# Latent attention: two transfers for the rows of a maximum in place of four, the first half's query rows shared by two queues, narrow maxima one slot later

## The reference

```python
Wdkv = x @ latent_w + latent_b                                   # [b, t, 36]: keys and values at once
q = jnp.einsum('btc,hcl->bhtl', x, Wd_w) + Wd_b[None, :, None, :]    # 16 heads, 36 wide
scores = jnp.einsum('bhtl,bsl->bhts', q, Wdkv) / sqrt(d_head)
scores = jnp.where(causal[None, None, :, :], scores, -jnp.inf)
attn = jax.nn.softmax(scores, axis=-1)
y = jnp.einsum('bhts,bsl->bhtl', attn, Wdkv)
return jnp.transpose(y, (0, 2, 1, 3)).reshape(b, t, h * 36) @ out_w + out_b
```

## Time and profile before

| what | value |
|---|---|
| median of 3 runs | 3344.71 us |
| the profiled execution | 3344.79 us, span 3343.1 us |
| PE busy | 2818.7 us (84%) |
| DVE busy | 2042.5 us (61%) |
| ACT busy | 1147.9 us (34%) |
| POOL busy | 805.4 us (24%) |
| stretch of the latent attention's pairs | 2143 to 3181 us |

### The profile page before, as it was taken

How to read it: one execution, slowest core, us unless ns; L and a number is a source line. 1 busy time by engine, 2 the same in 40 slices (tenths; PEclk the granted TensorE clock), 3 DMA queues, 4 the chain that set the end, 5 groups by cost and what they waited for, 6 DMA issues and landing times. The chain is left out here.

```text
span 3343.1 us, 53892 instructions
## 1 busy us (share of the span) xinstructions
PE 2818.7 (84%) x15208; PEld 1921.7 (57%) x15208; DVE 2042.5 (61%) x5177; ACT 1147.9 (34%) x2094; POOL 805.4 (24%) x1092
## 2 busy tenths in 40 slices
PE   5999999867888887799999988577887887787877
PEld 4777777644555555577777764334544454454453
DVE  6777777667777776677777763444544444454433
ACT  2111111146666665211111113244344433434332
POOL 1232232235555555222323210011001000000100
PEclk8999999968888888899999989688988888899888
DMA  3000000000000000200000000001001000101000
GB/s 124 0 0 0 0 0 0 1 1 2 3 2 3 2 2 3 92 0 0 0 0 0 0 1 0 27 28 34 23 26 30 28 23 28 33 23 32 23 1 25
DMA packets 31481, 52.02 MB, mean 16 GB/s; under 512 B 6914, under 2 KB 12290, under 8 KB 31236
## 3 DMA queue, kind: packets, MB, share of 16 engines
q1 hardware_dynamic: 31236, 48.96, 4.8%
HBM read 17.93 MB, written 2.10 MB: 6 GB/s over the span
## 5 line engine op out<-in xcount | busy, mean ns | idle before, releaser
L555 DVE SCALAR_TENSOR_TENSOR moe_acc<-moe_ps,moe_comb,moe_acc 128x512 f32<-128x512 f32 x896 | 661.2, 744 | 176.2 <-PE moe_ps L304 169.6
L2059 DVE CUSTOM_DVE_ANT_0 attn_masked<-attn_psm,attn_causal 128x1024 f32<-128x1024 f32 (+7 forms) x512 | 369.5, 756 | 456.3 <-PE attn_psm L1758 456.2
L1961 ACT ACTIVATE attn_probs<-attn_pse 128x512 f32<-128x512 f32 (+1 forms) x640 | 319.4, 554 | 470.6 <-PE attn_pse L1773 469.2
L304 PE MATMUL moe_ps<-moe_Wg,moe_xh 128*128 128x512 f32 x1024 | 329.9, 404 | 24.7 <-DVE moe_Wu L501 24.7
L335 PE MATMUL moe_ps<-moe_Wd,moe_ih 128*128 128x512 f32 x1024 | 337.9, 411 | 0.0
L304 PE MATMUL moe_ps<-moe_Wu,moe_xh 128*128 128x512 f32 x1024 | 337.6, 411 | 0.0
L1699 POOL TENSOR_SCALAR_AFFINE_SELECT attn_probs<-attn_probs 128x256 f32<-128x256 f32 (+1 forms) x192 | 94.6, 493 | 973.9 <-ACT attn_probs L1961 972.8
L1789 PE MATMUL attn_psy<-attn_probs,attn_V 128*64 128x512 f32 (+3 forms) x1536 | 328.2, 565 | 0.0
L1758 PE MATMUL attn_psm<-attn_kS,attn_qS 108*128 108x512 f32 (+3 forms) x672 | 214.2, 423 | 126.0 <-DMA attn_qS<-attn_qL 77.8
L454 POOL TENSOR_SCALAR moe_part<-consts,moe_pick,moe_prob 128x8 f32<-128x8 f32 x256 | 97.4, 395 | 753.6 <-ACT moe_prob L389 753.6
L1758 PEld LDWEIGHTS attn_psm<-attn_kS,attn_qS 108*128 108x128 f32 x672 | 123.0, 211 | 258.1 <-DVE attn_mx L2059 134.0
(11 more groups left out here) (208 smaller groups left out, 4747.4 us busy)
## 6 DMA issues: line engine op xcount, KB each, us to landing
attn_qS<-attn_qH SPq DMA_DIRECT2D x256, 72.0 KB
attn_qS<-attn_qL SPq DMA_DIRECT2D x128, 72.0 KB
moe_stageg<-in_w_gate SPq DMA_DIRECT2D x8, 512.0 KB, 7.0
moe_stageu<-in_w_up SPq DMA_DIRECT2D x8, 512.0 KB, 8.0
moe_stageg<-in_w_down SPq DMA_DIRECT2D x8, 512.0 KB, 3.6
out<-X SPq DMA_DIRECT2D x1, 2048.0 KB, 8.7
attn_qS<-attn_mh SPq DMA_DIRECT2D x64, 4.0 KB
attn_qS<-attn_ml SPq DMA_DIRECT2D x64, 4.0 KB
```

The costliest lines, as they stand in the source:

```text
L304: last = pe.matmul(expert_bank[j % 4][:, :], a[q][:, :], w[b][:, cols], start=k == 0, stop=k == 2)
L555: dve.scalar_tensor_tensor(acc[:, q, r, :], expert_bank[j % 4][:, :], comb[:, q, r, e:e + 1], acc[:, q, r, :], ALU.mult, ALU.add).then_inc ...
L1961: act.activation(probs[:, ring(q, u), c, HALF - n:HALF], e_part(k, HALF - n, HALF), ACT.Exp, scale=SCORE_SCALE).then_inc(p_ready, 1)
L2059: dve.tensor_tensor_reduce(masked[:, k % 2, 0:n], m_all[:, base:base + n], causal[:, SEQ - n:SEQ], 1.0, NEG, ALU.add, ALU.max, mx[:, q, v: ...
```

## The change

The two tiles `qS` of a pair's two heads become one tile with the heads side by side. With that one transfer carries a row of the maxima for both heads: two transfers instead of four, and the high row's is issued as soon as `mh` is there, ahead of the wait for `ml`. Of the six transfers of the first half, POOL issues the three of head 0 (at the place between its select of unit 8 and that of unit 9) and SP the three of head 1. The maxima are given a new order: slot 0 holds one wide maximum only, the narrow ones follow from slot 1 on, slot 3 holds two of them, and a maximum waits for the one before it of its own width, wherever that stands.

```diff
-        qS = [[sb(f"qS{q}{c}", [KROWS, SEQ], F32R) for c in range(2)] for q in range(2)]
+        qS = [sb(f"qS{q}", [KROWS, 2, SEQ], F32R) for q in range(2)]
...
-        QUERY_TILE = [8 * c + j for c in range(2) for wide, small in ((7, 1), (6, 2), (5, 3), (4, 0)) for j in (wide, small)]
+        WIDE = [(0, 7), (0, 5), (1, 7), (1, 5), (0, 6), (0, 4), (1, 6), (1, 4)]
+        NARROW = [(c, j) for j in (3, 2, 1, 0) for c in range(2)]
+        MAXIMA = [WIDE[0:1], (WIDE[1], NARROW[0]), (WIDE[2], NARROW[1]), (NARROW[2], WIDE[3], NARROW[3]),
+                  (WIDE[4], NARROW[4]), (WIDE[5], NARROW[5]), (WIDE[6], NARROW[6]), (WIDE[7], NARROW[7])]
...
+        def query_rows(eng, q, h, c, arrived):
+            s = HALVES[h]
+            half, rows = slice(s * HALF, (s + 1) * HALF), slice(c * LAT, (c + 1) * LAT)
+            for part, src in enumerate((qH, qH, qL)):
+                eng.dma_start(f32(qS[q][part * LAT:(part + 1) * LAT, c, half]), f32(src[q][rows, half])).then_inc(arrived, 16)
...
                 def maxima(m, q):
+                    sp.wait_ge(mh_ready, after(m))
+                    sp.dma_start(f32(qS[q][STACK:STACK + 1, :, :]), f32(mh[:, q, :])).then_inc(m_in, 16)
                     sp.wait_ge(ml_ready, after(m))
-                    for c in range(2):
-                        sp.dma_start(f32(qS[q][c][STACK:STACK + 1, :]), f32(mh[8 * c:8 * c + 8, q, :])).then_inc(m_in, 16)
-                        sp.dma_start(f32(qS[q][c][STACK + 1:STACK + 2, :]), f32(ml[8 * c:8 * c + 8, q, :])).then_inc(m_in, 16)
+                    sp.dma_start(f32(qS[q][STACK + 1:STACK + 2, :, :]), f32(ml[:, q, :])).then_inc(m_in, 16)
...
                 def queries(p, q, h):
                     sp.wait_ge(qs_ready, after(p * 2 + h))
-                    for c in range(2):
-                        rows = slice(c * LAT, (c + 1) * LAT)
-                        for part, src in enumerate((qH, qH, qL)):
-                            sp.dma_start(f32(qS[q][c][part * LAT:(part + 1) * LAT, half]), f32(src[q][rows, half])).then_inc(q_in[q][h], 16)
+                    for c in range(2) if h == 0 else (1,):
+                        query_rows(sp, q, h, c, q_in[q][h])
...
+                def first_queries(p, q):
+                    pool.wait_ge(qs_ready, after(p * 2 + 1))
+                    pool.sem_inc(pool_pause, 1)
+                    query_rows(pool, q, 1, 0, q_first[q])
...
                 def pair(m, i, b, more):
                     for u in DIAGONAL:
+                        if u == NU - 1 and follows(i, 2, more):
+                            pool.wait_ge(s_ready, after(m * NE + NE - 1))
+                            pool.sem_inc(pool_pause, 1)
+                            first_queries(m + 2, i % 2)
                         causal_part(m, i % 2, u)
...
-                    if n < 2:
-                        pe.wait_ge(q_in[q][n], (m - q) * 48 + 96)
-                    pe.wait_ge(mx_ready, after(m * 16 + n - 2))
+                    if before < 0 and j >= 4:
+                        pe.wait_ge(q_in[q][0], (m - q) * 48 + 96)
+                    elif before < 0:
+                        pe.wait_ge(q_in[q][1], (m - q) * 24 + 48)
+                        pe.wait_ge(q_first[q], (m - q) * 24 + 48)
+                    else:
+                        pe.wait_ge(mx_ready, after(m * 16 + before))
```

More of the change, by code:

```diff
@@ L1566, in attn1_phase @@
             sem("kp_ready"), sem("kt_ready"), sem("ks_ready"), sem("vp_ready"), sem("v_ready"))
+        q_first = [sem(f"q_first{q}") for q in range(2)]
         qp_ready, qt_ready, qs_ready, q_in = sem("qp_ready"), sem("qt_ready"), sem("qs_ready"), [[sem(f"q_in{q}{h}") for h in range(2)] for q in range(2)]
@@ L1582, in attn1_phase, with bank_before @@
         STEPS = NU // 2
-        QUERY_TILE = [8 * c + j for c in range(2) for wide, small in ((7, 1), (6, 2), (5, 3), (4, 0)) for j in (wide, small)]
+        WIDE = [(0, 7), (0, 5), (1, 7), (1, 5), (0, 6), (0, 4), (1, 6), (1, 4)]
+        NARROW = [(c, j) for j in (3, 2, 1, 0) for c in range(2)]
+        MAXIMA = [WIDE[0:1], (WIDE[1], NARROW[0]), (WIDE[2], NARROW[1]), (NARROW[2], WIDE[3], NARROW[3]),
+                  (WIDE[4], NARROW[4]), (WIDE[5], NARROW[5]), (WIDE[6], NARROW[6]), (WIDE[7], NARROW[7])]
+        IN_ORDER = [tile for slot in MAXIMA for tile in slot]
+        FIRST = [sum(len(slot) for slot in MAXIMA[:k]) for k in range(len(MAXIMA) + 1)]
+        def bank_before(n):
+            wide = IN_ORDER[n][1] >= 4
+            return max([k for k in range(n) if (IN_ORDER[k][1] >= 4) == wide], default=-1)
         def e_part(k, lo, hi):
@@ L1700, in causal_part, with start @@
                                        channel_multiplier=-1).then_inc(tri_ready, 1)
+                def first_queries(p, q):
+                    pool.wait_ge(qs_ready, after(p * 2 + 1))
+                    pool.sem_inc(pool_pause, 1)
+                    query_rows(pool, q, 1, 0, q_first[q])
+                def start():
+                    for p in range(2):
+                        first_queries(p, p)
+                    take_over(0)
                 def pair(m, i, b, more):
                     for u in DIAGONAL:
+                        if u == NU - 1 and follows(i, 2, more):
+                            pool.wait_ge(s_ready, after(m * NE + NE - 1))
+                            pool.sem_inc(pool_pause, 1)
+                            first_queries(m + 2, i % 2)
                         causal_part(m, i % 2, u)
-                pipeline(pool, lambda: take_over(0), pair, lambda b, more: take_over(b + 1) if more else None)
+                pipeline(pool, start, pair, lambda b, more: take_over(b + 1) if more else None)
             @block.tensor
@@ L1821, in maximum @@
                                 pe.wait_ge(v_ready, after(b + 1))
-                        for n in (2 * k, 2 * k + 1):
+                        for n in range(FIRST[k], FIRST[k + 1]):
                             scores_max(m + 1, 1 - q, n, keys)
@@ L1929, in high_query @@
                         if staged:
-                            act.wait_ge(q_in[i % 2][h], (p - i % 2) * 48)
+                            act.wait_ge(q_in[i % 2][h], (p - i % 2) * (24 if h else 48))
+                            if h:
+                                act.wait_ge(q_first[i % 2], (p - i % 2) * 24)
                         act.activation(qH[i % 2][:, s * HALF:(s + 1) * HALF], m_bank[h][0:2 * LAT, :], ACT.Identity,
```

23 lines of the change are left out of this document (10 added, 13 removed).

## The result

The changed kernel takes **3151.32 us** (median of 4 runs, 3144.09 to 3156.13) against 3347.55 us for the kernel before in the same job (4 runs, 3343.64 to 3353.79): a ratio of 0.941 with a 95% interval of 0.9385 to 0.9436, 196 us less. Measured again beside three variants it took 3150.59 us (5 runs). Both long waits went as forecast; two terms of the sum, the clock and the new order, were mis-sized.

A forecast was written before the change was run, and what follows sets the result against it. PE sets the pace (busy 828 of 1038 us), so only its waits can give time back. The terms -37 - 89 - 41 + 14 = -153 us against 3344.8 us gave 3191 us, range 3165 to 3255.

The forecast's parts named there:

- Two transfers for the maxima, -37: At a pair's first scores, PE's waits for the maxima's rows fall from 42.1 to some 4.8 us: -37 us.
- Query rows from two queues and the narrow maxima a slot later, -89: At the first narrow maximum, earlier rows and 2.3 us of moved work hide all 24 query-row waits: -89 us.
- A: POOL's transfers are dear: above 1.6 us each PE waits for unit 9's select; 3281 us, or 3322 at half clock; chance 0.17.
- D: Slower: POOL's transfers, at 4 us each, delay unit 9's select, values and exponents; 3442 us; chance 0.05.
- rival C: The second queue lands no query rows sooner; PE waits 1.2 us 24 times, about 3220 us; chance 0.07.
- The clock, -41: Work behind the query-row wait returns to full clock, 1.7 us for each of 24 waits: -41 us.
- The new order, +14: PE's waits for DVE in the reordered maxima grow by 0.5 us a pair over 28 pairs: +14 us.
- B: PE's clock does not come back because other waits remain in the pair: 3232 us; chance 0.08.
- The other rule weighed there: DVE's `low_query` might hold up POOL's three transfers until 2206.1 at worst; even then the forecast sum stays.

The follow-up runs named there:

- all but the two queues: The changed kernel with all six query transfers of the first half on SP: 3166.72 us, ratio 0.9465 to the kernel before.
- the memset: The changed kernel with a needless memset of 4096 columns (about 3.5 us) on POOL ahead of its three transfers: 3159.42 us, ratio 0.9452 to the kernel before.
- the queues alone: The kernel before with one `qS` tile and first-half query rows shared by POOL and SP, old order, four maxima transfers: 3278.35 us, ratio 0.9797.
- the order alone: The kernel before with one `qS` tile and the new order of maxima, all six query transfers on SP, four for the maxima: 3240.10 us, ratio 0.969.
- the filler: The kernel before with twelve needless products of 512 columns ahead of slot 0's narrow maximum, not in pairs 7: 3298.08 us, ratio 0.9864.
- the two transfers alone: The kernel before with one `qS` tile and two transfers for the maxima, old order, all query transfers on SP: 3279.97 us, ratio 0.9811.

## Why the prediction was wrong in size, step by step

**Two transfers for the maxima, -37.** Measured -34.1 (42.1 to 8.0). The mechanism is as forecast. The low row goes out 0.6 us behind the high one, but it lands later than the 1.88 us taken over from before: PE resumes 2.47 us behind its issue, and so 0.2 us of wait stay in many pairs where 0.3 were to spare. The trace gives a median of 2.3 us from its issue to its landing; without POOL's transfers beside it (all but the two queues) it is 1.8 us, and so it is where the memset moves them 3.5 us on; most pairs then have no such wait.

**Query rows from two queues and the narrow maxima a slot later, -89.** Measured -89.1: no such wait is left. POOL needs 0.51 us a transfer and not 0.77, which rules out rivals A and D; the memset shows how far they were off, 3.5 us of delay for 8 us. What the prediction gave for the queues without the order's cover, a wait of 1.2 us, is near what the queues alone show (0.9 to 1.2), though there SP still issued four transfers for the maxima; and what rival C gave for the order without a useful second queue, 1.2 us, is near what the order alone shows (1.37) and the change without the second queue (1.08).

**The clock, -41: this step failed in its size.** PE's busy time fell by 69.8 us for the same products. The forecast read the price, 1.7 us, off one wait, that of 3.77 us with 3.60 us of work at half clock behind it, and took it 24 times. That pair is among the cheapest. In the trace before, the half clock slid from the wait into the work behind it, from pair to pair. The pair that starts at 2543.74 us shows it, first the windows of its wait and of the work behind it, then PE's timeline:

```profile
2545.23:2548.99 3.76, 0.01 (x1) 0.01 (x1) 1.23 (x2) 0.71 (x2) 0.42 (x1) 0.91 0.28 81
2548.99:2554.99 6.00, 5.98 (x21) 3.59 (x21) 1.41 (x3) 1.74 (x4) 0.64 (x1) 0.50 0.00 0
```

```profile
2549.92 2.83 PE L1789 MATMUL attn_psy<-attn_probs,attn_V 128*64 128x384 f32 x12
2552.68 1.44 PE L1758 MATMUL attn_psm<-attn_kS,attn_qS 108*128 108x512 f32 x3
...
2555.17 0.98 PE L1758 MATMUL attn_psm<-attn_kS,attn_qS 108*128 108x512 f32 x3 [0.20 <-DVE attn_mx L2059]
```

PEclk was 0.91 over this wait, where it was 0.55 in the wait that was read, and half clock then stood over 6.0 us of work and not 3.6. In the eight ordinary pairs of the first two batch elements that have the same 103 or 104 products, PE's busy time rose from 23.00 us (the pair that was read) to 24.09; after the change it is 21.14 to 21.19 in all eight. The parts from one pair's first scores to the next's that hold one of the 24 waits lost 62.7 us of busy time, the others 7.0 us.

Part of the 62.7 us is no work. A row of the profile ends about 0.16 us behind the point where the next product can start (0.68 us for the two of slot 0 ahead of the wait in the earlier trace rows; after the change the next starts 0.52 behind them), and ahead of a wait this tail counts as busy; for the 53 vanished or shortened waits that is 8 us at most. At least 55 us are left, 2.3 us and more for each of the 24 and not 1.7.

**The new order, +14: this step failed too.** Measured over all the pairs, the waits for DVE changed by -1.7 us (45.6 to 43.9). Of its terms, slot 3's second narrow maximum was right (0.49 for 0.6), and so was slot 2 (0.54 for 0.73). Wrong was the charge of 0.2 us each for the narrow ones of slots 2 and 4, which do not wait at all, and slots 4 and 6 gained 0.5 us together and not 0.3. For the pair that was read that makes 1.26 us for 1.48, which would be -6 us in 28. It came to less because the 0.73 us of slot 2, too, was read where it was largest: over the ordinary pairs it ran from 0.74 down to 0.20 us (above), since DVE had caught up behind the longer half clock. Slower products thus hid part of their own cost in this wait.

Together: -34 - 89 - 70 + 0 = -193, against -37 - 89 - 41 + 14 = -153. The 40 us that the forecast lacked are 29 of busy time (clock above all), 14 of order, and 3 the other way. That idle time brings the clock down is shown by a kernel of its own, the filler; how the 69.8 us divide over the pairs is read from the two traces. Why the half clock slid from pair to pair was not tried and stays open.

**The rivals.** B, that the clock does not come back, was wrong for the whole change but largely true of each part: with the order alone or the queues alone, two waits that together make 2.6 to 3.4 us remain in a pair, and the clock still falls behind them in 14 of the 20 ordinary pairs. So a wait of 1.37 us at a PEclk of 1.00, which the prediction held against B, did not settle it, nor did the "over 3 us" that the expectation for the two transfers alone supposed. With the maxima's transfers and the order together PEclk is 1.00 in 18 of the 20, and with all three in all 20. C, that the second queue lands nothing sooner, is refuted by the queues alone: 89 us of waiting became 29. The Trainium skill (Trainium Kernel Development and Optimization, the item on the SP, ACT and POOL queues) says that a second issuer saves issue time only. The trace agrees: 1.52 us of POOL stand in for three steps of SP, and the only change in landing is the 0.5 us that `ml` lost (2.3 for 1.8). With the better cover of the order the second queue was worth 15 us.

The other rule weighed there, that GpSimd is kept from writing descriptors while DVE holds the shared port (the Trainium skill, SBUF — State Buffer, the box on the "DVE blocks DMA" trap), did not show. POOL's third transfer at 2201.42 lies for 0.38 us of its length beside DVE's `low_query` (2201.05 to 2201.80) and takes 0.51 us, as long as the first, from 2200.41, which lies ahead of it. No row tells whether `low_query` takes both ports, so this is no test of the rule itself.

The range was too narrow on its lower side: it allowed for 7 us from the opening and for the order at no cost, but it took the clock's price as a fixed 1.7 us a wait, off the one stretch that had been read in windows.

## What to carry to other kernels

Before pricing the clock off one wait, compare PE's busy time for the same products in every repetition of the stage: here it ran from 23.0 to 24.1 us, and the one read was at the cheap end. Price a reordering by each wait that it creates and by the slack ahead of it; a wait at one place pays for the next one on the same helper engine (1.1 us of waiting for rows cost 0.6 a pair, 3.5 us of delay on POOL 0.2). A list on one issuing queue is worth cutting and sharing only as far as PE's own work can't be put in front of it: the reordering alone gave 107 us, each of the others 67.

## What the runs showed of the hardware

- A transfer of 36 rows x 512 columns holds POOL for 0.51 us and SP for 0.71, and lands 2.0 to 3.4 us (median 2.1) behind its issue by POOL.
- One transfer of 16 source rows (8 KB) holds SP for 0.56 to 0.59 us, less than one of 8 rows did (0.63 to 0.66).
- Twelve products that nobody reads, put into a wait, made the kernel 47 us faster, since PEclk stayed at 1.00 in most pairs.
- Granted clock in the 20 ordinary pairs: with one wait of 1.1 us in a pair it stayed at 1.00 in 18; with two that together make 2.6 to 3.4 us it fell in 14, in the kernel with the order alone and in that with the queues alone.
- With the long wait of 3.8 us the half clock began at a different point of it from pair to pair: 3.6 us of work behind it ran at half clock in one pair, 6.0 in another.
- One row's transfer by SP landed 1.8 us behind its issue (median), and 2.3 us with POOL's three transfers issued beside it.
